# A graph and mixture-of-experts kernel: output zeroed in the second graph, raw rows in the token table

## The reference, cut to what matters

```
x = x + _L1_gnn_ref(_layernorm(x), W_u, b_u, W_v, src, dst)
# _L1_ffn_ref(_layernorm(x)[None], ...):
top_p, top_idx = jax.lax.top_k(softmax(xt @ Wr + br), 2)
weights = top_p / top_p.sum(axis=-1, keepdims=True)
xn = (xt - mu) * rsqrt(var + LN_EPS)            # a second norm, of the normed row
xe = xn * ln_g[e] + ln_b[e]
y = gelu(xe @ W1[e] + b1[e]) @ W2[e] + b2[e]    # 256 -> 1024 -> 256
out = sum over the two experts of weights * y   # and x + out is the result
```

## Time and profile before

| | |
|---|---|
| median of 3 runs | 4086.47 us (4084.59 to 4089.71) |
| the profiled execution: span of its instructions | 4086.3 us |
| second graph, first to last gather | 2009.0 to 3174.6 us |
| set-up block of the experts | 3192.5 to 3274.6 us |
| expert loop and end | from 3274.6 us |
| busy, whole span | PE 73%, DVE 56%, POOL 56%, ACT 32% |
| mean granted TensorE clock | 0.875 |

### The profile page before, as it was taken

One profiled execution on the slowest core, in us unless ns is written; L12 is line 12 of the kernel. 1 busy time (PEld: TensorE's weight loads), 2 busy tenths in 40 slices (PEclk: granted clock), 3 DMA queues, 4 the chain that ended last, 5 costly groups with the idle time before them and its releaser, 6 DMA issues. The chain is left out here.

```text
span 4086.3 us, 69498 instructions
## 1 busy us (share of the span) xinstructions
PE 2989.6 (73%) x12787; PEld 2168.3 (53%) x12788; DVE 2289.9 (56%) x5023; ACT 1298.0 (32%) x5485; POOL 2301.6 (56%) x2343
## 2 busy tenths in 40 slices
PE   4623777787878887999666665665656489999998
PEld 3422444444444444667544444444444378898887
DVE  4533888888888887874355555555555611111111
ACT  1401444444444454432211111111111533333343
POOL 5156777777777773002577777777777623333332
PEclk9866999899999998998777777778777789999999
DMA  8635444344444442000244444444444756666564
GB/s 188 193 89 147 116 116 117 105 108 108 108 107 109 110 111 62 0 2 30 75 112 113 113 112 113 112 113 113 113 112 112 220 173 166 170 174 167 167 172 128
DMA packets 292188, 487.96 MB, mean 119 GB/s; under 512 B 145315, under 2 KB 193393, under 8 KB 291625
## 3 DMA queue, kind: packets, MB, share of 16 engines
q0 software_dynamic: 127312, 325.41, 32.1%
q1 hardware_dynamic: 155936, 158.55, 13.2%
q10 hardware_dynamic: 8880, 3.34, 0.4%
HBM read 430.09 MB, written 57.50 MB: 119 GB/s over the span
## 5 line engine op out<-in xcount | busy, mean ns | idle before, releaser
L902 POOL DMA_INDIRECT g_rows<-rows,g_recs x1856 | 1764.1, 950 | 628.9 <-issue 474.1
L947 PE MATMUL g_pA<-g_msg,k_ident 128*128 128x264 f32 (+1 forms) x3712 | 1150.2, 463 | 474.0 <-DVE g_pA L1141 409.4
L947 PEld LDWEIGHTS g_pA<-g_msg,k_ident 128*128 128x128 f32 x3712 | 805.4, 228 | 803.8 <-issue 659.1
L936 PE MATMUL g_pE<-g_ew,g_recT 128*128 128x512 f32 x932 | 511.8, 676 | 251.3 <-DVEq L1125 248.4
L1135 DVE TENSOR_TENSOR g_msg<-g_rows,g_pp 128x1024 f32 (+3 forms) x464 | 571.9, 1233 | 151.2 <-DVEq L84 151.1
L1985 POOL DMA_INDIRECT out<-e_ys,e_goal x102 | 160.7, 1576 | 501.8 <-issue 481.1
L936 PEld LDWEIGHTS g_pE<-g_ew,g_recT 128*128 128x128 f32 x932 | 170.0, 202 | 468.9 <-DVEq L1125 343.1
L2038 PE MATMUL e_pY<-e_w,e_hT 128*128 x1632 | 373.8, 382 | 30.3 <-issue 30.3
L1057 ACT ACTIVATE g_pp<-g_dd 128x32 f32<-128x32 f32 x464 | 95.2, 205 | 921.0 <-ACTq L84 921.0
L2027 PEld LDWEIGHTS e_pH<-e_xT,e_w 128*128 128x128 f32 x3264 | 382.9, 193 | 5.2
L2027 PE MATMUL e_pH<-e_xT,e_w 128*128 128x128 f32 x3264 | 383.2, 276 | 0.0
(11 more groups left out here) (418 smaller groups left out, 3446.2 us busy)
## 6 DMA issues: line engine op xcount, KB each, us to landing
e_w<-in_L_ffn_W SPq DMA_DIRECT2D x110, 1024.0 KB
g_rows<-rows,g_recs POOLq DMA_INDIRECT x1856
g_recs<-slots SPq DMA_DIRECT2D x468, 8.0 KB
tok<-e_xall SPq DMA_DIRECT2D x7, 910.0 KB
rows<-p_row SPq DMA_DIRECT2D x50, 119.0 KB
own<-p_row SPq DMA_DIRECT2D x50, 119.0 KB
p_x<-in_x SPq DMA_DIRECT2D x1, 5600.0 KB
own<-p_x SPq DMA_DIRECT2D x1, 5600.0 KB
```

The lines of the kernel that those rows point to most:

```text
L902: pool.indirect_dma_start(out=rows[:, r, j, :], out_offset=None, in_=rows_d, in_offset=bass.IndirectOffsetOnAxis(ap=recs[:, r, 4 * j:4 * j ...
L936: last = t_.matmul(pE[:, c:c + 512], recT[:], ew[:].rearrange("p c d -> p (c d)")[:, c:c + 512], start=True, stop=True)
L947: last = t_.matmul(sums, K["ident"][:], of, start=False, stop=(j == C - 1), skip_group_check=True)
```

## The change

In the second graph SP's first ten cycles stand written out. After each it stores 640 KB of zeros (`blank`) to `out`, and loads one expert's second weights, or the norm's factors; b1 comes after the tenth. These buffers now live from before the graph. In the set-up block the rows of x go to the token table as they are, straight from `K["x"]`; the table's rows have eight more numbers instead of four, among them the factor and the offset of the double norm, written by one DMA of 32-byte records (`meta`). The 49 scatters of x to `out`, and POOL's wait for them, are gone. In the expert loop DVE's `keep` normalizes the gathered rows into `xn` (which PE turns), and prepares `yb` = first_of · x + weight · b2 in a ring of four (`YR`); `first_of` is 1 where this expert is the token's first, so x reaches `out` with the first expert's addition. After PE's outputs one DVE operation is left, outputs · weight + `yb`. `keep` of the tile two on now stands ahead of DVE's wait for the outputs of this one. DVE waits for b2 before it gives POOL the first row numbers.

```diff
 def graph(nc, K, ins, dr, layer, out=None):
...
+            ZT = 5
+            blank = m.sb(L + "blank", [P, ZT * D])
...
             @block.sync
...
-                with sp.Fori(0, n2 + (2 if first_layer else 1)) as u:
+                    sp.wait_ge(blank_ok, 1)
+
+                def cycle(u):
                     for r in range(R):
                         relay(u, r)
...
                         load(u + 1, r)
+                early = 0
+                if not first_layer:
+                    ZG = NT // ZT
+                    early = ZG
+                    for u in range(early):
+                        cycle(u)
+                        sp.dma_start(out.rearrange("(p g t) c -> p g (t c)", p=P, g=ZG)[:, u, :], blank[:]).then_inc(out_zero, 16)
+                        if u < X:
+                            sp.dma_start(K["w2"][:, u, :, :], ins["L1_ffn_W2"][u].rearrange("(k p) o -> p k o", p=128)).then_inc(ffn_in, 16)
+                        else:
+                            to, nm = ((K["gl"], "L1_ffn_ln_g"), (K["bl"], "L1_ffn_ln_b"))[u - X]
+                            sp.dma_start(to[:], ins[nm].rearrange("e (k p) -> p e k", p=128), allow_slow_non_contiguous=True).then_inc(ffn_in, 16)
+                    sp.dma_start(K["b1"][:], ins["L1_ffn_b1"].rearrange("e (k p) -> p e k", p=128), allow_slow_non_contiguous=True).then_inc(ffn_in, 16)
+                with sp.Fori(early, n2 + (2 if first_layer else 1)) as u:
+                    cycle(u)
...
+                    sp.wait_ge(out_zero, 16 * ZG)
+                    sp.wait_ge(ffn_in, 16 * (X + 3))
...
 experts, first block
...
                 def _(sp):
-                    for e in range(X):
-                        sp.dma_start(w2[:, e, :, :], ins["L1_ffn_W2"][e].rearrange("(k p) o -> p k o", p=128)).then_inc(w2_in, 16)
-                    for to, nm in ((gl, "L1_ffn_ln_g"), (bl, "L1_ffn_ln_b"), (b1, "L1_ffn_b1")):
-                        sp.dma_start(to[:], ins[nm].rearrange("e (k p) -> p e k", p=128), allow_slow_non_contiguous=True).then_inc(w2_in, 16)
+                    kept = dr["tok"][1:1 + NPAD, :].rearrange("(t q) c -> q t c", q=Q)
+                    for g in range(QT // GT):
+                        sp.dma_start(kept[:, g * GT:(g + 1) * GT, 0:D], x3[:, g * GT:(g + 1) * GT, :]).then_inc(tok_out, 16)
...
                     sp.wait_ge(meta_ok, 1)
-                    for g in range(QT // GT):
-                        sp.wait_ge(row_ok, GT * (g + 1))
-                        sp.dma_start(kept[:, g * GT:(g + 1) * GT, :], xall[:, g * GT:(g + 1) * GT, :]).then_inc(tok_out, 16)
-                    sp.wait_ge(tok_out, 16 * (QT // GT + 1))
-                    sp.wait_ge(w2_in, 16 * (X + 3))
+                    sp.dma_start(kept[:, :, D:XW], meta[:]).then_inc(tok_out, 16)
+                    sp.wait_ge(tok_out, 16 * (QT // GT + 2))
...
-                    for t in range(QT):
...
-                        s.activation(xall[:, t, 0:D], x3[:, t, :], ACT.Identity, bias=bias[:, t:t + 1],
-                                     scale=scale[:, t:t + 1]).then_inc(row_ok, 1)
...
+                    v.memset(meta[:], 0.0)
...
-                    for t in range(QT):
-                        q = QL if t == QT - 1 else Q
-                        pool.indirect_dma_start(out=out, out_offset=bass.IndirectOffsetOnAxis(ap=K["pt"][0:q, t, 0:1], axis=0),
-                                                in_=x3[0:q, t, :], in_offset=None).then_inc(x_out, 16)
-
-                    pool.wait_ge(x_out, 16 * QT)
...
 experts, second block
...
                         if not (isinstance(t, int) and t < 2):
-                            pool.wait_ge(xT_ps, t - 1)
-                            pool.sem_inc(pace, 1)
                             pool.wait_ge(kept, t - 1)
...
-                        pe.wait_ge(x_in[b], 16 * u + 16)
+                        pe.wait_ge(xn_ok, t + 1)
...
-                            last = t_.transpose(pX[:, k, :], xs[:, b, k * 128:(k + 1) * 128], K["ident"][:])
+                            last = t_.transpose(pX[:, k, :], xn[:, b, k * 128:(k + 1) * 128], K["ident"][:])
...
                     def keep(u, b):
...
                         dve.wait_ge(x_in[b], 16 * u + 16)
                         if not (isinstance(u, int) and u == 0):
                             dve.sem_inc(pace, 1)
+                            dve.wait_ge(xT_ps, t - 1)
+                            dve.sem_inc(pace, 1)
...
+                        v.tensor_scalar(xn[:, b, :], xs[:, b, 0:D], xs[:, b, D + 4:D + 5], xs[:, b, D + 5:D + 6], ALU.mult, ALU.add).then_inc(xn_ok, 1)
                         v.tensor_tensor(wsec[:, b:b + 1], xs[:, b, D + 2:D + 3], second[:, tc], ALU.mult).then_inc(wch, 1)
...
+                        v.tensor_scalar(row(yb[:, y, :]), xs[:, b, 0:D], first_of[:, tc], None, ALU.mult).then_inc(wch, 1)
...
+                        v.scalar_tensor_tensor(row(yb[:, y, :]), row(b2[:, bass.ds(e, 1), :]), wgt[:, y], row(yb[:, y, :]), ALU.mult, ALU.add).then_inc(kept, 1)
 
                     def group(u, first, last_group):
                         for b in range(2):
...
+                            if not last_group:
+                                keep(u + 1, b)
+                            dve.wait_ge(kept, t + 1)
...
                             dve.wait_ge(y_ok, t + 1)
...
-                            v.tensor_tensor(ys[:, b, :], pY[b][:], flat(b2[:, bass.ds(e, 1), :]), ALU.add).then_inc(sch, 1)
-                            v.tensor_copy(goal_b[b][:], goal[:, b:b + 1])
...
-                            v.tensor_scalar(ys[:, b, :], ys[:, b, :], wgt[:, b:b + 1], None, ALU.mult).then_inc(ys_ok, 1)
-                            if not last_group:
-                                dve.wait_ge(ys_ok, t + 1)
-                                dve.sem_inc(pace, 1)
-                                keep(u + 1, b)
+                            v.tensor_copy(goal_b[b][:], goal[:, y])
+                            v.scalar_tensor_tensor(ys[:, b, :], pY[b][:], wgt[:, y], row(yb[:, y, :]), ALU.mult, ALU.add).then_inc(ys_ok, 1)
+                    dve.wait_ge(b_in, 16)
                     for b in range(2):
                         v.tensor_copy(at[b][:], lst[:, b:b + 1]).then_inc(at_ok, 1)
```

More of the change, by code:

```diff
@@ L50 @@
 KC = HID // 128
-XW = D + 4
+XW = D + 8
+YR = 4
 class Chain:
@@ L783, in _, with graph @@
                 sp.sem_inc(stored, 1)
-def graph(nc, K, ins, dr, layer):
+def graph(nc, K, ins, dr, layer, out=None):
     first_layer = layer == 0
@@ L1107, in _ @@
                 v.memset(al[:], 0.0).then_inc(w_zero, 1)
+                if not first_layer:
+                    v.memset(blank[:], 0.0).then_inc(blank_ok, 1)
                 v.memset(accf[:], 0.0).then_inc(w_zero, 1)
@@ L1690, in experts @@
             x3 = K["x"]
[L1691 removed]
+            meta = m2.sb("e0_meta", [Q, QT, XW - D])
             GT = 7
@@ L2097, in _ @@
                     v = nc.vector
+                    row = lambda ap: ap.rearrange("p a c -> p (a c)")
                     def keep(u, b):
                         t = 2 * u + b
+                        e = expert(dve, t)
+                        y = bass.ds(t % YR, 1)
                         dve.wait_ge(x_in[b], 16 * u + 16)
@@ L2179, in program @@
         K["raw"] = m.sb("k_raw", [Q, 1 + QT, X])
-        graph(nc, K, ins, dr, 1)
+        K["w2"] = m.sb("k_w2", [128, X, KC, D])
+        K["gl"] = m.sb("k_gl", [128, X, 2])
+        K["bl"] = m.sb("k_bl", [128, X, 2])
+        K["b1"] = m.sb("k_b1", [128, X, KC])
+        graph(nc, K, ins, dr, 1, out)
         experts(nc, K, ins, dr, out)
```

59 lines of the change are left out of this document (25 added, 34 removed).

## The result

The changed kernel takes 4061.39 us (median of 4 runs, 4057.55 to 4062.25) where the kernel before takes 4085.53 (4 runs, 4081.34 to 4089.71): a ratio of 0.9939, 95% interval 0.9925 to 0.9953. That is 24 us less by the medians; 40 were forecast. The profiled execution of the change spans 4058.7 us, 27.6 less than that of before.

A forecast was written before the change was run, and what follows sets the result against it. Bounds: POOL's gather issue in the second graph, PE in the expert loop, stalled 0.93 us per pair by gathers. Sum: 4086.3 + 1 − 12.3 + 3.7 − 34 + 2 − 0.5 = 4046 us; own range 4034 to 4058, upper end taken to 4080.

The forecast's parts named there:

- Rival 2: Expert loop: half the slope of gather time against lead, -0.33 per pair, -15 in all, 4063 us; chance 0.13.
- Rival 3: Expert loop: DVE holds POOL's port, one issue per even pair 0.4 us later, +19, 4063 us; chance 0.07.
- Rival 4: Second graph pays: 160 gathers each 0.25 us longer, or POOL caught by late messages, +10 to +40; chance 0.05.
- Second graph, +1: Second graph: 160 of POOL's gathers issue slightly slower beside the added stores and loads, +1 us; bounds nothing and 10.
- Set-up block, -12.3: Experts' set-up block: scatters, weight loads and normalizations gone, DVE's lists end it, next block starts 12.3 us earlier.
- Start of the loop, +3.7: Loop start: DVE waits for b2 before the first row numbers, so the first gather starts later, +3.7 us; bounds 0.7 and 6.
- Loop, outputs to scatter, -0.50: Even pair, PE's outputs to scatter: DVE's two operations of 1.04 us become copy and one operation, 0.54; -0.50 us.
- Loop, the gather, -1.0: Even pair: gather leads the weight load by 0.64 us instead of 0.14, so it takes 4.7 us, -1.0.
- Loop, the new step, +0.67: Even pair: gathered rows pass through DVE before PE, two waits and one operation, +0.67 us.
- So I leave 0.2: Even pair: 0.2 us of the 0.93 stall kept for late gathers, so -0.73 per pair, 47 pairs, -34 us.
- POOL beside DVE, +2: Expert loop: three wide operations of `keep` may meet POOL's issues, +2 us (0.04 per pair); bounds 0 and 25.
- Rivals 1 and 5: Loop: 1, gather gets no shorter, 4087 us, chance 0.10; 5, landing bound to weight load, slower, 4109 us, chance 0.07.

The follow-up runs named there:

- the run in which PE waited for weights: The changed kernel, with SP starting each load of first-layer weights only once the rows of the tile after had landed: 4430.01 us, ratio 1.0837.

## Why the prediction was right in sign and short in size

The measured 4061 lies 3 us above the forecast's own range (4034 to 4058) and inside the stated one only because its upper end was taken to 4080 for rivals 2, 3 and 4. Of what the profile was to show, the block's length and the issue of the gathers came true (68.3 us where 69 to 70 were forecast, and still 1.25 us each); even pairs of 15.2 us (14.6 to 14.8 were forecast), gathers of 5.1 us (4.4 to 5) and a lead of 0.50 (0.6) did not. And of the 27.6 us between the two profiles 6.2 lie ahead of anything that the change touches: as far as these profiles stand for the runs, it is luck that the measured time lies no further from 4046.

- **Second graph, +1:** +0.6. SP's ten transfers of zeros and eight of weights cost POOL nothing: its 928 gathers take 1164.0 us, before 1164.7. Rival 4 is out.
- **Set-up block, -12.3:** -13.8. The end is DVE's last list operation, as forecast. I had taken 2.9 from ACT's normalizations, and 2.9 is what is left of the lists' 3.9 once the scatters' 1.0 is taken off. That 1.0 I had not seen: with the scatters gone DVE's lists are shorter by it; 0.8 of it are operations of DVE that take longer beside POOL's issues (below).
- **Start of the loop, +3.7:** +3.4, for the reason given. Taking the reason away gave 3.4 back.
- **Loop, outputs to scatter, -0.50:** -0.37. The last operation was taken at 0.42 and takes 0.48 (L2140), and the one-column copy ahead of it, with its wait for the scatter two tiles back, costs more than the 0.12 it was given: moved away together they gave 0.37.
- **Loop, the gather, -1.0:** -0.58. This is the term that was mis-sized. "From 0.14 to 0.54 the rows lose 1.2": it was read from one gather at 0.54, early in the loop, that took 4.9 us; the mean at a lead of 0.50 is 5.10. And I put the lead at 0.64 from an estimate of 0.50 for the step ahead of it. The measured slope to that point is 1.6 us per us of lead, not 2 to 2.5. Direction and mechanism were right (taken back in one run, stretched in another), but not a straight line.
- **Loop, the new step, +0.67:** +0.75.
- **"So I leave 0.2":** this is the step that failed. I took the stall as one number that would shrink until only scatter was left, and did not look for what would be late next. Even with the gather at the forecast 4.7 us DVE's own order is late: 0.41 per pair, 20 us over 49 pairs, that no shorter gather can win. The order of the instructions showed it before the run: `keep` stands behind the wide operation, and a number load stands at its head. The wait it adds for PE was priced by its length and not by when it can begin.
- **POOL beside DVE, +2:** nothing. Rival 3 is out: POOL's gathers in the loop take the same 0.98 us as before.
- **Rival 2** (half the slope) gave 4063, by a slope alone. The time is near the rival's, the mechanism half of it: a slope of two thirds of the forecast one, and a floor.
- **Rivals 1 and 5** are out: the gather got shorter, and a longer lead makes it still shorter.

The loop fell short by 21.6 us, 0.44 for each of the 49 pairs from tile 2 to 100: 15.20 measured (744.8 / 49) against 14.76 forecast (755.3 - 32 = 723.3, / 49). Of it 0.14 is the floor alone (14.90 against 14.76, 7 us) and 0.30 (15 us) are gathers that took longer than the floor hides.

## What to carry to other kernels

When a wait shrinks, ask before the run what the next latest input of the same engine is, and follow that chain with its own instructions; here a floor of 0.41 us per pair lay behind a stall of 0.93, and no earlier gather could have passed it. A small transfer that shares the DMA engines with a large one should be issued clearly ahead of it, and the profit is not proportional: against a lead of 0.13 us one of 0.50 gave 0.6 us and one of 1.13 gave 2.7. Cheapest of all was to reorder: POOL's gather ahead of its scatter, and a number load to where it is used, gave more than the change.

## What the runs showed of the hardware that was not expected

- The fall of the gather's time between leads of 0.50 and 1.13 us, from 5.10 to 2.96. The single gathers between put most of it between 0.7 and 0.9 us; no run had its leads there.
- POOL's issue of an indirect DMA can be stretched by DVE. In the set-up block of the kernel before, timeline of POOL and of DVE:

```profile
3234.80 0.96 POOL L1901 DMA_INDIRECT out<-k_x,k_pt  x1 [0.30 <-issue]
3236.07 1.77 POOL L1901 DMA_INDIRECT out<-k_x,k_pt  x1 [0.30 <-issue]
...
3235.08 0.93 DVE L1871 TENSOR_TENSOR e_at_hi<-e_iota_q,e_hi 128x742 f32<-128x742 f32 x1 [0.41 <-PE e_pL L1775]
3235.93 1.08 DVE L1872 TENSOR_TENSOR e_at_lo<-e_iota_q,e_lo 128x896 f32<-128x896 f32 x1
```

The issue that begins at 3236.07, inside DVE's 1.08 us operation on two SBUF inputs, takes 1.77 instead of 0.96. It is no single case: the six issues that begin 0.14 or 0.17 us into such an operation of L1872 take 1.75 to 1.78, the six that begin 0.53 us into one of L1871 (0.93 long) take 1.23 or 1.24, and the six inside which one of L1871 begins after 0.25 to 0.28 us take 0.96; these operations of DVE keep their length. Some short ones do not: the CAST of L1862 at 3219.60 takes 0.41 us beside POOL's issue and 0.19 in the kernel without scatters, and the 105 operations of the lists take 57.3 us in sum against 56.5. The Trainium skill (SBUF: State Buffer, "Who interferes with whom") states such a lock between a DVE operation with two SBUF inputs and a GpSimd instruction that reads SBUF; these rows agree. The same section infers that a `tensor_tensor` leaves the making of DMA descriptors alone; the issues of 1.77 us speak against that, and the measurement decides. It was in the trace before the prediction, which said that no row of the followed pair prices an overlap: it had looked only in the loop. In the loop of the changed kernel it does not come up, as the source view of the gathers says:

```profile
L1975 POOL DMA_INDIRECT e_xs<-tok,e_at x97: 979/982/996, 3293.1 to 4023.4; - x97
```

- By the chain the matmuls of the outputs take 3.72 us behind a gap of 0.15 us or more and 3.46 without, so a short stall of PE costs 0.26 more than its length. Of it 0.16 is overlap with the group ahead that is lost, and 0.10 is a longer group.
- In the run in which PE waited for weights (busy for 522 of 700 us) its granted clock was 0.87 in the loop, a mix of both levels; in the changed kernel (680 of 700) it was 1.00, that is 2.4 GHz. PE had stood for 6.66 us before it began the hidden layer at 3320.72; the granted clock was 0.52 from 3319 to 3326 us, nearly all at 1.2 GHz, and the 32 matmuls took 6.37 us instead of 3.73. From 3326 to 3343 us it was 1.00 again. So such a wait costs more than its length.
